# A graph kernel's edge stage: duplicates summed within half-batches of seven columns, halves loaded in an interleaved order, keys fetched at another place, zeros written in strips

## The reference

```python
deg = jax.ops.segment_sum(ew, col, num_segments=N) + 1.0     # ew = clip(abs(edge_weight), 1e-6)
agg = jax.ops.segment_sum(dis[row] * ew * dis[col] * xw[row], col)   # GCN, two layers
...
m = h @ weight[i]                                             # GRU, five rounds
agg = jax.ops.segment_sum(m[src] * edge_attr[:, None], dst)   # edge_attr = edge_weight
```

## Time and profile before

| | us |
|---|---|
| runs | 3556.3, 3559.46, 3566.68 (median 3559.46) |
| the profiled execution's own time | 3565.2 |
| its span, first to last instruction | 3563.6 |
| first scatter to `plane_a` starts | 107.81 |
| first scatter to `plane_w` starts | 880.76 |
| last scatter to `plane_w` starts | 1949.44 |

### The profile page before, as it was taken

One profiled execution on the slowest core, in us unless ns is written; L12 is line 12 of the kernel. 1 busy time (PEld: TensorE's weight loads), 2 busy tenths in 40 slices (PEclk: granted clock), 3 DMA queues, 4 the chain that ended last, 5 costly groups with the idle time before them and its releaser, 6 DMA issues.

```text
span 3563.6 us, 53452 instructions
## 1 busy us (share of the span) xinstructions
PE 3037.7 (85%) x18088; PEld 2735.1 (77%) x18089; DVE 2290.7 (64%) x4691; ACT 1568.7 (44%) x3207; POOL 1423.4 (40%) x934
## 2 busy tenths in 40 slices
PE   2655444699999399996898999999999999999898
PEld 1545444588888389995798889889988998899777
DVE  4999999678788656666554455555555555555556
ACT  1554455444455233334543444444444444444355
POOL 1488888888888456667887000000000000000000
PEclk8555555699999699998999999999999999999889
DMA  9888798767766633525654443334333333333110
GB/s 324 316 232 234 217 254 253 177 170 165 203 180 151 183 104 104 179 51 146 187 130 90 135 135 129 117 126 130 129 117 121 126 126 128 125 129 117 40 39 25
DMA packets 403604, 538.64 MB, mean 151 GB/s; under 512 B 148349, under 2 KB 305828, under 8 KB 399972
## 3 DMA queue, kind: packets, MB, share of 16 engines
q1 hardware_dynamic: 275374, 484.68, 40.4%
q0 software_dynamic: 118944, 18.55, 8.7%
q10 hardware_dynamic: 9110, 33.10, 3.0%
HBM read 398.99 MB, written 137.25 MB: 150 GB/s over the span
## 4 chain that ended last, share of the span: by engine, by line
PE 41%; POOL 5%; DVE 3%; issue 1%; ACT 1%; DMA 0%; SPq 0%; POOLq 0%; ACTq 0%; DVEq 0%
PE bank L673 40%; POOL plane_w L551 5%; PE bank L852 1%; DVE ring_lo L1851 0%; ACT ring_hi L1225 0%; DVE gates_sb L1877 0%; DVE gates_sb L1876 0%; DVE xT L1878 0%; ACT nat_b L1326 0%; DVE v_lo L1908 0%; PE bank L916 0%; DMA fb<-in_L_ffn_b1T 0%; DMA ring_lo<-plane_w 0%; ACT v_hi L1284 0%; DVE res_b L1970 0%
## 5 line engine op out<-in xcount | busy, mean ns | idle before, releaser
L551 POOL DMA_INDIRECT plane_a<-pair,slot x392 | 630.7, 1609 | 239.2 <-issue 118.2
L551 POOL DMA_INDIRECT plane_w<-pair,slot x392 | 666.8, 1701 | 124.9 <-issue 118.7
L673 PE MATMUL bank<-ring_hi,h_hi 128*128 128x448 f32 x1750 | 651.8, 372 | 56.5 <-DVE ring_lo L1851 51.1
L1851 DVE TENSOR_TENSOR ring_lo<-ring_lo,ring_hi 128x448 fp32r<-128x448 f32 x875 | 522.9, 621 | 237.5 <-ACT ring_hi L1225 237.1
L1225 ACT ACTIVATE ring_hi<-ring_lo 128x448 fp32r<-128x448 f32 x875 | 496.8, 576 | 395.0 <-PE bank L673 373.4
L673 PE MATMUL bank<-ring_lo,h_hi 128*128 128x448 f32 x1750 | 642.7, 367 | 0.0
L673 PE MATMUL bank<-ring_hi,h_lo 128*128 128x448 f32 x1750 | 642.6, 367 | 0.0
L602 POOL DMA_DIRECT2D v_lo<-gru_v x4 | 3.0, 754 | 1080.3 <-PE bank L673 1080.3
L673 PEld LDWEIGHTS bank<-ring_hi,h_hi 128*128 128x128 f32 x1750 | 330.8, 189 | 85.8 <-DVE h_lo L1918 38.5
L1869 DVE SCALAR_TENSOR_TENSOR gates_sb<-bank,bhh,gates_sb 128x448 f32<-128x448 f32 x70 | 47.9, 684 | 521.1 <-ACT gates_sb L1249 521.1
L673 PEld LDWEIGHTS bank<-ring_hi,h_lo 128*128 128x128 f32 x1750 | 330.5, 189 | 27.8
(11 more groups left out here) (384 smaller groups left out, 6613.1 us busy)
## 6 DMA issues: line engine op xcount, KB each, us to landing
ring_lo<-plane_w SPq DMA_DIRECT2D x175, 1120.0 KB, 5.4
gring_lo<-plane_a SPq DMA_DIRECT2D x50, 1280.0 KB
plane_w<-nat SPq DMA_DIRECT2D x100, 400.0 KB
plane_a<-nat SPq DMA_DIRECT2D x25, 1344.0 KB, 36.6
w_hl<-w_split SPq DMA_DIRECT2D x16, 2048.0 KB
xT<-in_L_ffn_W SPq DMA_DIRECT2D x32, 512.0 KB, 7.5
w_split<-xT SPq DMA_DIRECT2D x32, 512.0 KB, 5.9
w_split<-nat SPq DMA_DIRECT2D x32, 512.0 KB, 6.9
```

The costliest lines, as they stand in the source:

```text
L551: g_.indirect_dma_start(out=plane, out_offset=bass.IndirectOffsetOnAxis(slot[:, t:t + 1], 0), in_=pair[:, k, t:t + 1], in_offset=None, com ...
L673: last = mm(ps, lhs[x], rhs[y], start=start and n == 0, stop=stop and n == 2)
L1851: V.tensor_tensor(ring_lo[:, t, :], ring_lo[:, t, :].bitcast(FP32), ring_hi[:, t % HS, :].bitcast(FP32), ALU.subtract).then_inc(lo_rdy, 1)
```

## The change

- **Compares within halves.** A column is compared with the columns of its own half only; PE sums within halves (56 small matmuls for 105).
- **Loading order.** The halves of the sorted list are put at positions 0, 2, 4, 1, 6, 3, 8, 5, ... 52, 49, 54, 51, 53, 55 (position: which half stands there). POOL scatters positions in order. Each half now reads a number of `apart` and starts when the half two places earlier has landed, and the one before it too, unless their destinations don't overlap.
- **Loads.** Six DMAs for each tile instead of three; `edge_weight` goes over ACT's queue.
- **Keys.** The first two key loads stand right behind the write of `key_rows`; `mark_low(0, 0)` stands ahead of `keep_v(0)`.
- **Zeros.** The 2688 columns are written as three strips of 896 (75 pieces of 448 KB); the pieces of `plane_w` wait for landed halves of `plane_a`'s scatters, 12 for each batch from the second on.

```diff
-UP = G * (G + 1) // 2
-FB, B0 = 8, 3
+FB, B0 = 12, 2
+NH = 2 * NB
+UPH = GH * (GH + 1) // 2
+UP = 2 * UPH
+EH = GH * EP
+WIDE = (NP - STRIP) // 3
+STRIPS = 1 + 3 * NT
...
+        first_of = lambda q: q // GH * GH
+        eq_at = lambda q, x: (q // GH * UPH + q % GH * (q % GH + 1) // 2 + x - first_of(q)) * EP
...
+        def load_edges(eng, tile, v):
...
+            eng.dma_start(to[:, 0:2, :], halves[:, 0:3:2, :]).then_inc(edges_in, 16)
+            eng.dma_start(to[:, 2:NH - 3:2, :], halves[:, 4:NH - 1:2, :]).then_inc(edges_in, 16)
+            eng.dma_start(to[:, 3:NH - 2:2, :], halves[:, 1:NH - 4:2, :]).then_inc(edges_in, 16)
+            eng.dma_start(to[:, NH - 2, :], halves[:, NH - 3, :]).then_inc(edges_in, 16)
...
+            load_edges(sp, dsti, "dst")
+            load_edges(sp, srci, "src")
...
-            for t in range(NT):
-                sp.dma_start(adj_a[t * 128:(t + 1) * 128, STRIP:NP], diagonal(t)[:, STRIP:NP]).then_inc(filled_a, 16)
+            for lo in range(STRIP, NP, WIDE):
+                for t in range(NT):
+                    sp.dma_start(adj_a[t * 128:(t + 1) * 128, lo:lo + WIDE], diagonal(t)[:, lo:lo + WIDE]).then_inc(filled_a, 16)
             for n in range(FW * NT):
-                sp.wait_ge(placed, B0 + n // FB + 3)
+                sp.wait_ge(scat_a[1], LANDED * (B0 + n // FB))
...
+            def begin_half(p, landed):
+                h = p % 2
+                if p >= 2:
+                    pool.wait_ge(landed[h], LANDED * (p // 2))
+                if p >= 1:
+                    pool.wait_ge(landed[1 - h], pool.value_load(apart[0:1, p - 1:p], min_val=LANDED, max_val=LANDED * NB))
                     hold(pool)
...
-                    for q in range(g + 1, G):
-                        mm(ps_sum[c][:, g, 0:6], eq_row(c, q, g, g + 1), parts(q, 6), start=False, stop=(q == G - 1))
+                    for q in range(g + 1, first_of(g) + GH):
+                        mm(ps_sum[c][:, g, 0:6], eq_row(c, q, g, g + 1), parts(q, 6), start=False, stop=(q % GH == GH - 1))
...
+            act.wait_ge(padded, 4)
+            load_edges(act, w, "edge_weight")
...
-            keep_v(0)
             act.wait_ge(keyT_out, 16)
...
             for b in range(KB):
-                load_keys(b, b)
+                load_keys(b, b, False)
...
+            mark_low(0, 0)
+            keep_v(0)
             keep_v(1)
-            mark_low(0, 0)
...
+            go(V.tensor_tensor(far[:, 0, 0:NH - 1], turns_of[:, 1, 1:NH], turns_of[:, 0, 0:NH - 1], ALU.is_gt))
+            go(V.tensor_tensor(far[:, 1, 0:NH - 1], turns_of[:, 1, 0:NH - 1], turns_of[:, 0, 1:NH], ALU.is_gt))
...
+            go(V.tensor_scalar(apart[:, :], far[:, 0, :], float(LANDED), None, ALU.max))
...
-                    if q > 0:
-                        V.tensor_scalar(eq_row(c, q, 0, q), keyrow[b][:, 0:q * EP], at(key, q), None, ALU.is_equal, ALU.add, accum_out=before_n[:, c, q:q + 1])
+                    if q % GH:
+                        V.tensor_scalar(eq_row(c, q, first_of(q), q), keyrow[b][:, first_of(q) * EP:q * EP], at(key, q), None, ALU.is_equal, ALU.add, accum_out=before_n[:, c, q:q + 1])
```

More of the change, by code:

```diff
@@ L532, in _, with scatter @@
                 g_.memset(limits[:, GCH + c:GCH + c + 1], float((c + 1) * GW)).then_inc(consts, 1)
[L534 to L538, removed]
-                    hold(pool)
-            def scatter(plane, k, n, landed):
-                b, r = divmod(n, G)
-                h = 1 - r // GH
-                if r == 0:
-                    if b > 0:
-                        pool.wait_ge(landed[1], LANDED * b)
-                    far_enough(b, landed[0])
-                if r == GH and b > 0:
-                    pool.wait_ge(landed[0], LANDED * b)
-                t = G * b + GH * h + r % GH
+            def begin_half(p, landed):
[4 more added lines that the diff above has]
+                    pool.wait_ge(landed[1 - h], pool.value_load(apart[0:1, p - 1:p], min_val=LANDED, max_val=LANDED * NB))
+                    hold(pool)
+            def scatter(plane, k, t, landed):
+                p = t // GH
+                if t % GH == 0:
+                    begin_half(p, landed)
                 g_.indirect_dma_start(out=plane, out_offset=bass.IndirectOffsetOnAxis(slot[:, t:t + 1], 0),
-                                      in_=pair[:, k, t:t + 1], in_offset=None, compute_op=ALU.add).then_inc(landed[h], 16)
+                                      in_=pair[:, k, t:t + 1], in_offset=None, compute_op=ALU.add).then_inc(landed[p % 2], 16)
             def scatter_w(n):
@@ L633, in _ @@
             for m in range(2):
-                last = tr(bank[1][0:NB, m * 128:(m + 1) * 128], ends[:, m, :], ident[:, :])
+                last = tr(bank[1][0:NH, m * 128:(m + 1) * 128], ends[:, m, :], ident[:, :])
             last.then_inc(keyT_ps, 1)
@@ L1471, in _ @@
             link(V.reduce_max(needed[:, :], under[0:1, :, :], AX))
-            go(V.scalar_tensor_tensor(far[:, 2:NB], far[:, 2:NB], -float(LANDED), after_turn[:, 2:NB], ALU.mult, ALU.add))
+            link(V.tensor_tensor(far[:, 0, :], far[:, 0, :], far[:, 1, :], ALU.max))
+            go(V.scalar_tensor_tensor(far[:, 0, :].rearrange("p (b h) -> p b h", h=2), far[:, 0, :].rearrange("p (b h) -> p b h", h=2), -float(LANDED),
+                                      turns[:, :].rearrange("p (b h) -> p b h", h=1).to_broadcast([1, NB, 2]), ALU.mult, ALU.add))
```

62 lines of the change are left out of this document (34 added, 28 removed).

## The result

The changed kernel runs in 3542.55 us (median of 6 runs, 3535.05 to 3545.46), against 3561.24 us before in the same comparison: a ratio of 0.9949, 95% interval [0.9933, 0.9966]. It is faster, by 19 us. The forecast was 3515: direction right, and the gain less than half of what was forecast. The profiled execution took 3545.46 us with a span of 3543.9.

A forecast was written before the change was run, and what follows sets the result against it. DVE's batches bound the kernel, then POOL's scatters once those end 10 to 15 us earlier; a 15th scatter 45.0 us earlier brings the second layer 43.6 earlier: 3565.2 - 44 = 3521, median 5.7 lower, 3515; range 3494 to 3548.

The forecast's parts named there:

- The first scatter: POOL's first scatter to plane_a, after edges, keys, two compares, products and place: forecast at 72.5 us against 107.81.
- edges, I take 3: Edge loading at the start: edge_weight on the other queue releases DVE 3 us earlier, between 0 and 6.
- a term of 0: The skill's reading of the edge loads: a second queue gains nothing, leaving the time 3 us later, at 3518.
- Keys asked at 23.4 plus 16.7: First key loads: asked for at 23.4 us and landed 16.7 us later, at 40.1, just when DVE is ready.
- The landing waits: POOL ahead of the 8th and 15th scatter: 5.5 us each, kept between 0 and 20.4; 15th scatter at 109.4.
- The scatters' pace: POOL's 378 scatters to plane_a: 1.92 us each, unchanged, so the gain is the 15th scatter's time, 45.0 us earlier.
- Chunk seven has its data at 844: End of the first GCN layer: chunk seven's data at 844, it takes 24.2 us, second layer at 875.3.
- the first (landings stay slow): Rival at POOL's start: both landing waits take 20.4 us, second layer at 905, time 3546; chance 0.12.
- The second (zeros in small pieces hold the fifth batch): Rival on zero strips: each piece pays its landing, strips end at 297, fifth batch waits 110 us, 3619; chance 0.04.
- The third (no change): Rival on DVE: weight parts hold the batches, PE starts the GCN at 676.71 still, time 3560; chance 0.07.
- fourth: Rival of more gain: products and landings cost nothing, 15th scatter at 91.5, 55 to 60 us, near 3500; chance 0.09.
- at about 353: Gate of the plane_w zeros: ten landed second halves, so MoE weight parts begin near 353 us instead of 404.80.

The follow-up runs named there:

- late_keys: Changed kernel with the first key loads and marks put back behind the products' evictions, as before the change; 3549.42 us, ratio 0.9967 to the kernel before.
- keys_only: Kernel before the change with only the early key loads and ACT's first marks ahead of the products; 3556.06 us, ratio 0.9985.
- weights_on_sp: Changed kernel with the six edge_weight loads moved from ACT's queue to SP's, behind the other twelve; 3527.71 us in one run.
- one_strip: Changed kernel with the 2688 columns of zeros as one strip (rows of 10752 bytes) instead of three; 3560.01 us, ratio 1.0003 to the kernel before.
- six_strips: Changed kernel with the 2688 columns of zeros as six strips (rows of 1792 bytes) instead of three; 3533.77 us, ratio 0.9908 to the kernel before.
- full_compares: Changed kernel with compares and sums over the whole batch again, the rest kept; 3535.53 us, ratio 0.9932 to the kernel before.
- best_full: all_three with compares and sums over the whole batch again; 3536.88 us, ratio 0.9928 to the kernel before.
- after_again: The changed kernel run once more, unaltered, as a yardstick; 3541.59 us, ratio 0.9936 to the kernel before.
- all_three: Changed kernel without the two first landing waits, with products behind the first batch's sums and the padding half not last; 3515.85 us, ratio 0.9877.

## Why the forecast went wrong

The mechanism was right: POOL's list of scatters bounds the second layer, compares and sums beyond that are hidden behind it, and PE waits ahead of chunks five to seven (17.17, 39.94 and 3.41 us). Compare (11.07 us, forecast 10.95), first chunk (585.36, forecast 580 to 625) and last `place` (568.98, not after 609) came as worked out. The size failed: the second layer was forecast at 875.3 and came at 894.13, 18.8 us later, the sum of four terms. That is most of the 27.6 us by which the median missed; 4.8 went behind the GRU (below), and the rest is rounding and the median's distance from the profiled execution, 2.9 us where I took 5.7.

- **The first scatter, 77.00 for 72.5: 4.5 us.** The step "edges, I take 3" took credit for the second queue and none of the cost of twice as many loads: DVE was released 1.0 us later than before, not 3 earlier, and the weights behind those loads came at 50.08 for 45.3. Two runs take the two apart: with the six loads and no early keys (late_keys) the products start at 45.45, 2.0 later than before, and with early keys and the old loads (keys_only) at 47.97, 4.5 later, near the 4.8 I had for the keys. The chain from there (products, evictions, `mark_low`, copy, `place`) ran as written. On the second queue the Trainium skill, "DMA: Bandwidth & Descriptors", section "Issuing engines are not separate DMA queues", says that only issue time is saved; the trace agrees in that 2.1 us was saved, of the 5.8 that SP takes to issue these six loads in weights_on_sp (14.24 to 20.08). My reading of it as a term of 0 was also off. "Keys asked at 23.4 plus 16.7" was wrong without harm: they landed before DVE was ready.
- **The landing waits, 8.26 and 9.29 for 5.5 each: 6.4 us.** This is the largest term. I took the price from a wait that stood beside no zeros. Its two ends, 0 and 20.4, held it; one_strip and six_strips show that the width of the zeros' rows moves it.
- **The scatters' pace, 1.937 for 1.921: 5.6 us over 378.** "Nothing in the change makes one shorter" was true, but the weight parts and the GCN's loads now run beside more of them. That these slow them is argued from when the pace rises (1.875 in the second 56 scatters, 2.015 in the sixth 56, beside the GCN). It was 1.912 to 1.924 in the four kernels whose GCN starts after 649 (before, keys_only, full_compares, best_full), and 1.926 or more in all others. No run of its own shows it; in `after_again` the pace was 1.926 and the term some 2 us, so part of it is this execution's.
- **The end of layer one, 2.3 us.** "Chunk seven has its data at 844" priced the way from the last scatter to PE at 10.35 us; it was 17.1 (850.46 to 867.56), since the padding half lands late (10.11 us, below). The interleaved order moved that half to the end of the list, and I had not followed which edges stand there. PE waited 3.41 us for it, and chunk seven then took 26.6 us, not 24.2: its first 2.5 us ran at a granted clock of 0.50 (1.2 GHz), where before, without such a wait, it was 1.00 (2.4 GHz). Chunk six gave back some 3.3: it began 1.9 us sooner after the scatters than worked out and took 32.6 us for the 34 that I allowed. The landing, then chunk seven's first 2.5 us after and before the change (window, its length, PE busy and matmuls, granted clock):

```profile
850.46 10.11 DMA plane_a<-pair,slot
```

```profile
867.50:870.00 2.50, 2.44 (x11) 0.50 0.57 165
```

```profile
894.70:897.20 2.50, 2.49 (x21) 1.00 0.92 258
```


From the second layer to the GRU the gain of 24.7 stayed at 24.5, but only because POOL's last scatter came 31.5 us earlier and the same late landing took 7.0 of it. Why POOL gained 6.7 us there is open (from the second layer to the last scatter 1030.6 us before, 1023.9 after, 1019.3 to 1027.8 in the other kernels). From the GRU to the end 4.8 us more went in this execution (below), which the forecast had at 0; over the other kernels of the table this stretch (the span's end less the GRU's start, 1603.8 us before, 1608.6 after) ran from 1599.1 (keys_only) to 1612.4 (six_strips) and follows no edit.

Of the rivals, the first (landings stay slow) came true by about a fifth, 17.6 us in two waits for the forecast's 11 or its 40.8. It would have put the second layer at 905. The second (zeros in small pieces hold the fifth batch) did not occur in the changed kernel, but not by the margin I gave: I put the end of the strips at 140, and in all_three POOL waited for them until 183.99. I had given the zeros the whole rate and left out the keys, the products' writes and the scatters that share it (from 140 to 150 us in the changed kernel ACT's queue had 43.7% of the engines' time and POOL's 9.7%). In that rival the 1.05 us of data for a piece of 448 KB should be 1.2 at 0.38 MB/us, which changes nothing. The third (no change) and fourth fell: the first chunk came before 625, and the first scatter and the landings cost more than I had, not less. The gate "at about 353" is 351 by its own working, also without effect.

## What to carry to other kernels

When two chains reach the same place nearly together, 186 us of saved work on one is worth what the other leaves; price that other chain's waits first, since its small terms decide. A scatter's landing time depended here on the rows of what shared the DMA engines: try splitting long rows before moving small scatters beside them, and do not price a landing from a quiet stretch. When a change reorders a list, look at which item is last now, and whether it is a slow one.

## What the runs showed of the hardware

- **Late landing of padding.** The half with 176 padding elements, which go to neighbouring words, landed 7.8 to 10.6 us after its last scatter's start, other halves 2.9 to 3.1. In the changed kernel the queue moved nothing from 1922 to 1926, and the landing came at 1926.61. DMA queues from 1920 to 1927 us (each digit is the busy share of a slice of 0.175 us, in tenths):

```profile
DMA  0000099531000000000000000000000000000000
...
q0 software_dynamic: 144, 0.00, 8.3%
```

  That neighbouring addresses are the reason is my guess; the runs show only that the half with the padding is the late one.
- **Same clock, two paces.** PE in the GRU's rounds (window, its length, PE busy and matmuls, granted clock): before, the first, second and last whole round; after, the last two. The last two columns are the DMA share and GB/s.

```profile
2062.00:2394.80 332.80, 328.45 (x1605) 1.00 0.38 124
2394.80:2722.30 327.50, 323.22 (x1604) 1.00 0.39 126
...
3049.60:3325.20 275.60, 272.67 (x1345) 1.00 0.34 111
```

```profile
2693.70:3022.60 328.90, 324.64 (x1605) 1.00 0.39 125
3022.60:3303.50 280.90, 278.02 (x1344) 1.00 0.34 109
```

  The same 1605 matmuls took 332.8 or 327.5 us, the last round 275.6 or 280.9, at a granted clock of 1.00 and with 4.3 us of idle time in each of the first two. Which round is slow differs between these two executions. Why is open, and so is how much of the spread between runs it makes.
